# Transposed scores and exponentials two slots behind the scores in an attention and expert kernel

## What is computed

```python
x = x + tanh(g_xattn[0]) * attention(layernorm(x), ctx, ctx)     # causal, 16 heads, softmax over keys
x = x + tanh(g_ffn[0]) * experts(layernorm(x))                   # 8 experts, the 2 best of each token
```

## Time and profile before

| | us |
|---|---|
| median of 3 runs | 938.75 |
| range of the runs | 936.92 to 939.47 |
| the profiled execution, its own time | 942.84 |
| its span, first to last instruction | 940.9 |
| TensorE busy in the span | 846.5 (90%) |
| VectorE busy | 600.4 (64%) |
| ScalarE busy | 442.3 (47%) |
| GpSimd busy | 257.6 (27%) |

### The profile page before, as it was taken

How to read it: one execution, slowest core, us unless ns; L and a number is a source line. 1 busy time by engine, 2 the same in 40 slices (tenths; PEclk the granted TensorE clock), 3 DMA queues, 4 the chain that set the end, 5 groups by cost and what they waited for, 6 DMA issues and landing times. The chain is left out here.

```text
span 940.9 us, 24425 instructions
## 1 busy us (share of the span) xinstructions
PE 846.5 (90%) x7600; PEld 750.5 (80%) x7601; DVE 600.4 (64%) x1521; ACT 442.3 (47%) x962; POOL 257.6 (27%) x239
## 2 busy tenths in 40 slices
PE   3599999999999999999539999999999999999990
PEld 2488888888888888888338789998989998989980
DVE  2357888888888888887636555555555555555540
ACT  2155555655555555654224444554444455544440
POOL 3001333222332333323210322232332232223332
PEclk9699999999999999999659999999999999999996
DMA  8765666665667787864388432323233233322222
GB/s 185 141 135 132 158 152 129 139 155 156 155 159 202 188 185 176 174 164 156 130 288 295 87 53 48 54 53 53 48 50 52 48 59 50 51 48 36 30 24 25
DMA packets 87944, 108.77 MB, mean 116 GB/s; under 512 B 12832, under 2 KB 81568, under 8 KB 85664
## 3 DMA queue, kind: packets, MB, share of 16 engines
q1 hardware_dynamic: 72448, 87.17, 37.4%
q0 software_dynamic: 14304, 19.15, 12.7%
q10 hardware_dynamic: 1088, 1.11, 0.4%
HBM read 46.82 MB, written 34.36 MB: 86 GB/s over the span
## 5 line engine op out<-in xcount | busy, mean ns | idle before, releaser
L1220 POOL DMA_INDIRECT out_rows<-yg,xs x78 | 126.6, 1624 | 332.7 <-ACT yg L1262 190.3
L1352 PE MATMUL bank<-xh,wts 128*128 128x256 f16 x1872 | 214.2, 275 | 0.0
L1368 PE MATMUL bank<-wts,hh 128*128 x1872 | 210.6, 273 | 0.0
L1352 PEld LDWEIGHTS bank<-xh,wts 128*128 x1872 | 185.0, 99 | 22.5
L1368 PEld LDWEIGHTS bank<-wts,hh 128*128 128x128 f16 x1872 | 183.2, 98 | 21.2
L1252 ACT ACTIVATE hf<-bank,b1t,gscale 128x256 f32<-128x256 f32 x312 | 154.7, 562 | 24.3 <-PE bank L1352 24.3
L979 PE MATMUL bank<-va,probs 128*128 128x102 f32 x1024 | 139.7, 278 | 8.1 <-DVE ao L696 8.1
L979 PEld LDWEIGHTS bank<-va,probs 128*128 128x128 f32 x1024 | 124.2, 192 | 10.7 <-DVE ao L696 6.2
L1262 ACT ACTIVATE yg<-yb,xs 128x256 f32<-128x256 f32 x78 | 35.4, 500 | 199.5 <-DVE yb L1301 199.5
L583 ACT ACTIVATE probs<-bank 128x512 f32<-128x512 f32 x128 | 76.9, 601 | 101.8 <-PE bank L962 95.2
L1291 DVE SCALAR_TENSOR_TENSOR hh<-hf,hscale,hh 128x512 f16<-128x512 f32 x156 | 117.1, 751 | 5.6
(11 more groups left out here) (169 smaller groups left out, 1082.0 us busy)
## 6 DMA issues: line engine op xcount, KB each, us to landing
wts<-in_W SPq DMA_DIRECT2D x16, 1024.0 KB, 7.9
wts<-keys SPq DMA_DIRECT2D x96, 128.0 KB
wts<-queries SPq DMA_DIRECT2D x96, 128.0 KB
xs<-token_rows SPq DMA_DIRECT2D x39, 272.0 KB
split_weights<-wts SPq DMA_DIRECT2D x8, 1024.0 KB, 4.6
wts<-split_weights SPq DMA_DIRECT2D x8, 1024.0 KB
xin<-in_x SPq DMA_DIRECT2D x16, 256.0 KB, 4.0
cin<-in_ctx_in SPq DMA_DIRECT2D x16, 256.0 KB, 4.2
```

The costliest lines, as they stand in the source:

```text
L1220: pool.indirect_dma_start(out=out[:, :], out_offset=bass.IndirectOffsetOnAxis(ap=numbers, axis=0), in_=yg[m % 2][:, half, :], in_offset=No ...
L1352: last = pe.matmul(HB[c // 2][:, c % 2 * TILE:(c % 2 + 1) * TILE], wts[:, bass.ds(expert[1], 1), at:at + P], xh[b][:, xp, k, :], start=q = ...
L1368: last = pe.matmul(YB[b][:, half * D:(half + 1) * D], hh[b][:, hp, c, half * P:(half + 1) * P], wts[:, bass.ds(expert[0], 1), at:at + D], ...
```

## The change

On ScalarE and TensorE, the exponential and ST of quad m move from slot m + 1 to slot m + 2: in slot n they now take quad n - 2, and in slots 0 and 1 quads 6 and 7 of the group before. PV stays in slot m + 3, and S, the maximum and all else stay where they were. No wait is edited: the waits of lines 745, 894, 952, 953, 579, 582 and 969 name the same quads as before.

```diff
@@ -574,7 +574,7 @@
-                        q, pg = (QUADS - 1, g - 1) if n == 0 else (n - 1, g)
+                        q, pg = (QUADS + n - 2, g - 1) if n < 2 else (n - 2, g)
                         if there(pg):
                             act.wait_ge(st_psum, pg * QUADS + q + 1)
 
@@ -945,9 +945,9 @@
-                        if there(g if n >= 1 else g - 1):
-
-                            tg, m, i = (g, n - 1, par) if n >= 1 else (g - 1, QUADS - 1, p1)
+                        if there(g if n >= 2 else g - 1):
+
+                            tg, m, i = (g, n - 2, par) if n >= 2 else (g - 1, QUADS + n - 2, p1)
                             tok = slice((m // 4) * P, (m // 4) * P + P)
                             pe.wait_ge(max_ready, tg * QUADS + m + 1)
```

## The result

The changed kernel takes 956.79 us (median of 4 executions, 953.47 to 958.17) against 939.04 us for the kernel before: a ratio of 1.0188 [1.0158 to 1.0219]. It is slower by 1.9%, outside the range of 937.0 to 943.6 us. The profiled execution took 957.11 us, its span is 955.2 us. An execution more than 1.5% above the fastest of its kernel is left out of times and ratios; this is so for one alone, the profiled execution of `e14_before_norm6_thin4`.

The account below looks back on a forecast made before the run. TensorE was taken as the bound, with VectorE pacing part of slots 4 to 7. Terms 0 + 0.3 + 0 + 0.9 = +1.2 us on the median of 938.75 gave 940.0 us, range 937.0 to 943.6.

Parts of the forecast that it names:

- The hole ahead of ST: Slot 7: ST's 0.43 us wait goes, PV(4)'s wait grows from 0.54 to about 1.0 or 1.2 us; gain 0.
- the same chain of VectorE: Unbroken VectorE work from slot 4's output product to `ao`, 6.07 us, said to set the pace up to PV(4).
- The chain from `k_rest` to the end of `ao`: VectorE from slot 1 to PV(0) of slot 3: 6.43 us without a gap, starting 0.95 us later.
- the wait of PV(0): Last group, slots 0 to 3: VectorE's late maximum moves `ao` and PV(0); 0.9 us taken, bounds 0 to 1.0.
- The restacked keys: SyncE's key transfers wait for a later last ST and slip some 0.35 us, before S needs them; cost 0.
- clock: Rival: slot 6 and 7 holes become one per group, bringing half-speed stretches; 949.8 us (every second group) or 958.2; 10%.
- overrun: Rival: VectorE's chain from slot 1 delays PV(0) of slot 3; 0.3 us a group gives 943.6 us; 12%.
- a gap of 1.47 us: Last group, TensorE: its stretch was granted clock 1.00, taken as evidence that long gaps need not lower the clock.
- the two holes of slot 7: TensorE idles 0.43 us ahead of ST and 0.54 us ahead of PV(4); read as one hole paced by VectorE.
- The margin of 0.00 us: PV(0) of slot 3: cover for late `ao` falls from 0.95 us to nothing; 0.3 us taken, bounds 0 to 2.0.
- the modelled end of ST: Slots 0 and 1: the waiting maximum was put 0.03 us after ST ends, 0.89 us late in slot 0.

Follow-up runs that it names:

- e14_before_norm6_thin4: Kernel before, with the first sequence's normalise in slot 6 and 4 unread 8-column matmuls behind the joined slot-7 hole: 965.47 us, ratio 1.0274.
- e4_split_max4: Changed kernel with four rowmax buffers instead of two, and slot-7 ST also waiting for the maximum of quad 6: 941.23 us, ratio 0.9988.
- e5_before_norm6: Kernel before, with the first sequence's normalise moved from slot 7 to slot 6, ahead of that slot's maximum: 941.59 us, ratio 1.0012.
- e11_fill_behind: Changed kernel with 8 unread 256-column matmuls behind PV(4) in slot 7, between the hole and the narrow products: 958.5 us, ratio 1.0192.
- e7_norm6_max4: Changed kernel with the first sequence's normalise moved to slot 6 and four rowmax buffers: 944.33 us, ratio 1.0069.
- e13_before_norm6_wide: Kernel before, with the first sequence's normalise in slot 6 and 8 unread 256-column matmuls behind the joined slot-7 hole: 953.98 us, ratio 1.0121.
- e1_split: Changed kernel with one more wait: in slot 7 ST also waits for the maximum of quad 6: 946.67 us, ratio 1.0055.
- e2_fill: Changed kernel with 8 unread 256-column matmuls in slot 7, in the hole ahead of PV(4): 945.52 us, ratio 1.0042.

## Why the prediction was wrong

**What held.** The hole ahead of ST brought no gain: its wait moved to PV(4), 1.16 to 1.25 us in each group where 1.0 to 1.2 was foreseen, behind the same chain of VectorE. The chain from `k_rest` to the end of `ao` in the group at 275.79 is 283.29 to 289.72, the 6.43 us of the sum. In the last group the wait of PV(0) went from 1.47 us to 2.15, 0.7 where 0.9 was taken. The restacked keys came in time: S has no wait for them in a middle group. Without clock and overrun the order costs nothing (`e4_split_max4`).

**The step that failed: the clock.** The sum had no term for it; it stood as a rival at 10%, with 949.8 us if every second group were hit. The pattern came, nearly every second group (six of 13), at 1.7 us for each stretch where 1.4 was put. What spoke against it in the text was that TensorE's idle time in a group stays the same, and that a gap of 1.47 us was not followed by half clock while one of 1.37 us was the earlier trace rows. Both looked at idle time alone. Idle time alone did not decide: 1.05 us without half clock (`e5_before_norm6`), the hole of the changed kernel without (`e11_fill_behind`), 0.75 us with (`e7_norm6_max4`). The gap ahead of the first S of group 1 was 1.37 us in the kernel before, with half clock behind it, and is 1.52 us in the changed kernel, without. The reading that fits the runs: the change took ST from between the two holes of slot 7, so that both now lie as one close ahead of the narrow products. The rows of slot 7 behind PV(4), which are listed as busy, were not weighed in the prediction.

The Trainium skill (TensorE: Matmul & The Clock Gate, Part 1) says that activity releases the throttle. `e13_before_norm6_wide` and `e14_before_norm6_thin4` agree with it in part: 1.05 us of wide and 1.06 us of narrow products are equally busy in the profile, and only behind the wide ones did the clock stay full in every middle group.

**The term that was mis-sized: PV(0).** The margin of 0.00 us was rightly found for the group that was read, its price was not: 0.3 us with a bound of 2.0, where 2.8 us came (`e1_split` against `e4_split_max4`, 345.25 and 342.43 us). Two pieces made it, and the timeline has both. The lag of the maximum behind the modelled end of ST is 0.13 us (282.16 + 0.39 = 282.55, and 282.68), not 0.03, and that is the 0.10 us of the group shown. And the chain of 6.43 us was read in one group, one of only three of the 13 (8, 9 and 14) in which it is so short. In the other ten it holds a short wait inside the routing and takes 6.65 to 6.73 us, in the kernel before as in the changed one. The changed kernel's timeline of VectorE in the group at 302.38:

```profile
311.52 0.87 DVE L675 SCALAR_TENSOR_TENSOR k_rest<-bank,bqk,keys 128x256 f32<-128x256 f32 x2
...
316.79 0.17 DVE L815 COPY all_slots<-slots 128x16 int32 x1 [0.18 <-DVE slots L811]
...
317.82 0.42 DVE L696 TENSOR_TENSOR ao<-bank,rden 128x256 f32<-128x256 f32 x1
```

The list of waits between 60 and 460 us has the same row in the kernel before and in the changed one:

```profile
DVE all_slots L815 <- DVE slots L811: 1.3, 8, 0.2
```

In that group `k_rest` to the end of `ao` is 6.72 us (311.52 to 318.24) and PV(0) waits 0.27 us. The waits of the 13 groups, 0.10 us in the three and 0.20 to 0.27 us in the ten, make some 2.75 us, near the 2.8 us of the two runs. The rival "overrun" named this place at 0.3 us a group, 943.6 us, and gave it 12%: near the right price (0.21 us a group), with too small a chance.

**The two together.** Taking the rivals one at a time left out that both can come: 10.2 + 2.8 = 13.0 us, which is what the middle groups grew by. The medians of the two kernels are 17.8 us apart, the profiled executions 957.11 - 942.84 = 14.3; the profiled execution of before lay 3.8 us above its median, and where the other executions save that is not traced.

## What to carry to other kernels

Before moving work on TensorE, look at what will stand beside each hole as well as at how long it is: with narrow products next to a hole of about 1 us the clock fell where it did not with wide ones, and one stretch at half clock (1.7 us) cost more here than one hole (1.2 us). A slot's margin is to be read over all groups of a loop, not in one, above all when it comes out as zero. And a hole that waits for another engine's chain is no room to be won: where one was closed here by moving work, most of its time came back at another product that waits for VectorE or ScalarE.

## What was not expected of the hardware

- TensorE's granted clock fell, in part of the groups, behind holes of 0.57 to 1.25 us where products of 4 to 8 columns lay close to them, and not behind one of 1.05 us with wide products next to it. With wide products alone around it, it fell in five of seven cases at 2.15 to 2.54 us and in none of nine at 1.27 to 1.76 us.
- 4 narrow float32 matmuls cost 1.5% more than 8 wide bf16 ones of the same 1.05 us (1.0274 against 1.0121), and 8 narrow ones, which last twice as long, 58 us more (1012.01 against 953.98 us).
- Adding 0.9 us of unread work to each group made the changed kernel faster: its ratio to the kernel before fell from 1.0188 to 1.0042 (`e2_fill`), its middle groups from 355.05 to 345.24 us.
